# Order of the row maxima and the products with V, in the units that follow a shift

## What is computed

```python
xn = jax.nn.silu(group_norm(x, gn_scale, gn_offset))
qkv = jnp.einsum('bxyc,cd->bxyd', xn, w_qkv)
q, k, v = jnp.split(qkv, 3, axis=-1)          # then to 8 heads of 64 channels
q = q * HEAD_CH ** (-0.5)
sim = jnp.einsum('bhdi,bhdj->bhij', q, k)
attn = jax.nn.softmax(sim, axis=-1)
out = jnp.einsum('bhij,bhdj->bhid', attn, v)  # then heads back to channels
out = jnp.einsum('bxyd,dc->bxyc', out, w_out) + b_out
return out + x
```

## Time and profile before

| | us |
|---|---|
| median of 3 runs (4330.1 to 4330.94) | 4330.39 |
| the profiled execution | 4330.27 |
| its span, from the first to the last instruction | 4328.5 |
| TensorE busy in it | 3827.5 (88%) |
| VectorE busy | 3022.1 (70%) |
| ScalarE busy | 2851.5 (66%) |
| GpSimd busy | 1717.7 (40%) |
| mean granted clock of TensorE | 0.958 |

### The profile page before, as it was taken

How to read it: one execution, slowest core, us unless ns; L and a number is a source line. 1 busy time by engine, 2 the same in 40 slices (tenths; PEclk the granted TensorE clock), 3 DMA queues, 4 the chain that set the end, 5 groups by cost and what they waited for, 6 DMA issues and landing times.

```text
span 4328.5 us, 90413 instructions
## 1 busy us (share of the span) xinstructions
PE 3827.5 (88%) x32844; PEld 2133.3 (49%) x32844; DVE 3022.1 (70%) x3936; ACT 2851.5 (66%) x3202; POOL 1717.7 (40%) x1226
## 2 busy tenths in 40 slices
PE   3889999898998989989899998989989899898997
PEld 1445545454554545545455454545545455454553
DVE  5676676867767676676766768677676766767664
ACT  2676676767767676676766767667676766766664
POOL 1243443433434343343434434334343333434333
PEclk8989999999999999999999999999999999999999
DMA  2111112122021121212111121220311212121111
GB/s 75 37 38 47 57 30 74 31 59 60 16 82 36 50 55 32 73 30 59 45 47 57 30 74 31 59 59 16 82 37 50 55 31 74 30 59 45 40 54 36
DMA packets 105031, 211.25 MB, mean 49 GB/s; under 512 B 13392, under 2 KB 13392, under 8 KB 104656
## 3 DMA queue, kind: packets, MB, share of 16 engines
q1 hardware_dynamic: 104656, 205.84, 17.8%
HBM read 71.57 MB, written 33.55 MB: 24 GB/s over the span
## 4 chain that ended last, share of the span: by engine, by line
PE 52%; DVE 19%; issue 16%; ACT 4%; POOL 4%; SPq 2%; DMA 2%; DVEq 1%; POOLq 0%; ACTq 0%
PE SD L891 27%; PE PV L1004 9%; DVE Pl L760 5%; DVE mx L707 5%; PE TP L905 5%; PE ST L971 4%; PE ST L970 4%; POOL Pl L460 3%; SPq L353 2%; DVE work L750 2%; ACT QK L521 2%; DMA work<-in_x 1%; PE TP L912 1%; ACT Ph L562 1%; PE SD L947 1%
## 5 line engine op out<-in xcount | busy, mean ns | idle before, releaser
L559 ACT ACTIVATE P<-ST,cns 128x1024 f32<-128x1024 f32 x1024 | 1142.0, 1115 | 753.6 <-PE ST L971 536.3
L460 POOL TENSOR_TENSOR Pl<-P,Ph 128x1024 f16<-128x1024 f32 x512 | 1212.0, 2367 | 920.4 <-ACT Ph L562 917.3
L707 DVE TENSOR_REDUCE mx<-TP 128x1 f32<-128x1024 f32 x1024 | 1248.3, 1219 | 234.0 <-PE TP L905 223.8
L562 ACT ACTIVATE Ph<-ST,cns 128x1024 f16<-128x1024 f32 x1024 | 1134.8, 1108 | 0.0
L1004 PE MATMUL PV<-V,Ph 128*128 128x129 f16 (+2 forms) x10240 | 893.7, 213 | 133.9 <-DVE Pl L760 122.8
L1004 PEld LDWEIGHTS PV<-V,Ph 128*128 128x128 f16 x10240 | 790.6, 99 | 385.0 <-DVE Pl L760 150.7
L1004 PE MATMUL PV<-V,Pl 128*128 128x65 f16 x8192 | 861.9, 195 | 0.0
L970 PE MATMUL ST<-QK 128*128 128x512 f16 x2048 | 807.3, 394 | 0.4
L971 PE MATMUL ST<-QK 128*128 128x512 f16 x2048 | 807.1, 394 | 0.0
L1004 PEld LDWEIGHTS PV<-V,Pl 128*128 128x128 f16 x8192 | 740.1, 100 | 89.7 <-issue 17.1
L905 PE MATMUL TP<-QK 128*128 128x512 f16 x2048 | 640.6, 396 | 105.4 <-DVE QK L711 53.8
(11 more groups left out here) (91 smaller groups left out, 2889.6 us busy)
## 6 DMA issues: line engine op xcount, KB each, us to landing
QK<-QK SPq DMA_DIRECT2D x384, 256.0 KB, 4.8
work<-in_x SPq DMA_DIRECT2D x128, 256.0 KB, 2.8
res<-in_x SPq DMA_DIRECT2D x128, 256.0 KB, 2.8
out<-res SPq DMA_DIRECT2D x128, 256.0 KB, 2.0
V<-in_L_conv_w_qkv SPq DMA_DIRECT2D x1, 3072.0 KB, 10.4
P<-in_L_conv_w_out SPq DMA_DIRECT2D x1, 1024.0 KB, 12.3
bias<-in_L_conv_b_out SPq DMA_DIRECT2D x1, 256.0 KB, 7.4
gam<-in_L_conv_gn_scale SPq DMA_DIRECT2D x1, 2.0 KB, 12.0
```

What stands on the lines that cost most here:

```text
L460: nc.gpsimd.tensor_tensor(Pl[:, v % 4, :], P32[:, v % 2, :], Ph[:, v % 4, :], ALU.subtract).then_inc(lo_pool, 1)
L559: nc.scalar.activation(P32[:, v % 2, :], ST[:, v % 2, :], ACT.Exp, scale=cns[:, 0:1])
L562: nc.scalar.activation(Ph[:, v % 4, :], ST[:, v % 2, :], ACT.Exp, scale=cns[:, 0:1]).then_inc(exp_done, 1)
L707: nc.vector.reduce_max(mx[:, hh, qb:qb + 1], TP[:], AX.X).then_inc(top_drained, 1)
```

## The change

The order on TensorE is turned round in the units for which `shift_before` gives a shift, that is, where the unit before ended with one. There TensorE now does the products with V of unit v-2 first and the row maximum of v behind them. Nothing is added or removed, and no other engine's program is touched: `shift_before` is an existing function (L72).

```diff
@@ -1012,11 +1012,14 @@
                     before = (b, v - 2) if v >= 2 else (b - 1, UNITS + v - 2)
                     scores(b, v, 0, cnt)
                     scores(b, v, 1, cnt)
-                    for use in unit_max(s, u, last):
+                    maxima_first = not shift_before(s, u, last)
+                    for use in unit_max(s, u, last) if maxima_first else []:
                         top_use(use, image_of_tops(b, s, u), cnt)
                     if not (first and v < 2):
                         times_v(*before, 0, cnt)
                         times_v(*before, 1, cnt)
+                    for use in [] if maxima_first else unit_max(s, u, last):
+                        top_use(use, image_of_tops(b, s, u), cnt)
                     for use in side_uses(s, u, first, last):
                         side(use, image_of(use, b, s), cnt)
                     for use in unit_shift(s, u, last):
```

## The result

The changed kernel takes 4722.82 us (median of 4 runs, 4712.88 to 4724.11), against 4330.25 us for the kernel before in the same comparison: a ratio of 1.090, with a 95% interval of 1.088 to 1.092. It is 392 us slower. I had forecast 93 us.

The account below looks back on a forecast made before the run. The prediction took the slackless chain of row maximum, reduction, low part and next products as the bound; 15 images at 5.6 us (84 us) plus 9 us for image 15 made 93 us, forecasting 4423 us, range 4385 to 4452.

Parts of the forecast that it names:

- What bounds the kernel: Chain from TensorE's row maximum through VectorE's reduction and low part to TensorE's next products, claimed to have no slack.
- The gain of a plain unit and the 0.62 us: Plain unit: TensorE's 0.09 us wait for the shift copy goes; row maximum and reduction come 0.62 us later.
- The sum: All units together: 5.6 us in each of images 0 to 14, 9 us in image 15, together 93 us.
- unit 23: Would pay 0.62 us, but a 4.77 us wait for an image block two units on takes it up: 0.
- units 43 and 44: Unit 43, at half clock: products end about 0.4 us late, minus 0.25 of slack, counted as +0.2 us.
- Unit 39: Products fit in front of the row maximum's 1.82 us wait for the late shift copy; counted as -0.69 us.
- It ends 0.62 us later.: VectorE's low part of v-1, in order behind the delayed reduction, was claimed to end 0.62 us later.
- units 15 and 35: A projection covers the delay; unit 15 has 2.0 us of slack and gains 0.09 us, unit 35 counts nothing.
- The bounds of the unit's price: Price per delayed unit: at least 0.53 us (79 us in all), at most 0.71 us (106 us).
- the rival: TensorE's clock: lengthened waits add half-clock time, 24 us, giving 4447; chance 0.23 for the clock to either side.
- Faster: Wait for the shift copy goes and the later reduction costs nothing: 53.8 us gained, 4276; chance 0.06.
- nothing measurable: Waits elsewhere (load, placement, statistics) take up the delays; time stays at 4330; chance 0.05.

Follow-up runs that it names:

- turns_on_after: Changed kernel plus a wait: in units with v % 4 = 3 GpSimd's low part starts only after VectorE's of the unit before; 4367.08 us, ratio 1.009.
- turns_on_before: Kernel before plus a wait: in units with v % 4 = 3 GpSimd's low part starts only after VectorE's of the unit before; 4276.91 us, ratio 0.988.
- turns_only_unit7: Kernel before with GpSimd's low part waiting for VectorE's low part of the unit before in unit 7 of each image alone; 4276.9 us, ratio 0.988.

## Why the prediction was wrong

**What bounds the kernel.** Right. The chain (row maximum, reduction, low part, products of the next unit) was the one that decided, and it had no slack.

**The gain of a plain unit and the 0.62 us.** Right. The row maximum starts 1.57 us into the unit and the reduction 2.20, and the next products come 4.62 us behind the start where no turn is lost.

**The sum.** 93 us forecast, 90 us measured, as the difference between `turns_on_after` and `turns_on_before`. That it is so close is partly luck: the sum held the clock as it was, but the clock moved between the two (see below), and the four runs of `turns_on_after` lie 15 us apart. The single units are the better test, by the scores' starts in the two traces, as means over images 1 to 14. Without units 25 and 26 and 33 to 35, where the load wait and stretches at the lower level fall, an image is 6.1 us longer; the sum gives 6.2 for the same units, with unit 23 at 0.62. With all units it is 4.8 us, where I had 5.6. Units 47 and 48 together keep their length, the delay of unit 23 is taken up by the wait for the image block in unit 25, and units 43 and 44 together lose 0.14 us (I had 0.2). Unit 39 gave 0.46 us, not 0.69.

**The step that failed** is this one: "It ends 0.62 us later." I moved VectorE's low part by 0.62 us and kept its duration at 1.22 us. A duration from a row holds only as long as the instruction meets the same neighbours. Here it started 0.08 us behind GpSimd's in place of 0.53 us ahead, and took 3.12 us in place of 1.22. That is 1.9 us more in eleven units of an image. In units 15 and 35 most of it is hidden by a projection, and in unit 23 the wait for the image block takes it up. The other eight pay it: 8 x 16 x 1.9 = 243 us. Unit 15 still pays 0.65 us, 10 us in all. In image 15 all sixteen low parts of these units are long, and the image is 41 us longer, not the 15 counted here, a part of it by the clock. The runs give 4722.8 - 4367.1 = 356 us for all of it. The rest goes in the main with TensorE's clock, as the next point but one argues.

**The bounds of the unit's price** were therefore too narrow. I bounded it by 0.53 and 0.71 us, both from TensorE's rows, and asked only how long others would wait for VectorE. What VectorE itself would wait for inside an instruction was not in the list. The trace of the kernel before had it twice: the low part of GpSimd at 2.68 us in place of 2.12 just behind VectorE's, and the copy of V at 3.17 us. The first has no term in my sum, and I counted the copy as a fixed link in unit 7.

**The clock.** With the turns set right the granted clock was 0.968 in the old order and 0.978 in the new one, 82 us fewer at the lower level, worth up to 41 us. So the order in itself did not bring more of the lower level, although it lengthens ten gaps an image, and the rival was wrong as I had put it. The 90 us above are the order's price less what this gave back. The gaps of lost turns did bring more. The changed kernel has 0.949, that is (1 - 0.949) x 2 x 4721.5 = 482 us in the lower state, against (1 - 0.978) x 2 x 4356.9 = 192 us with the turns set right. Those 290 us are worth up to 145, enough for the 100 us or so that unit 15 and the eight leave open; that they fill it exactly isn't shown. Unit 4 is such a place; in the changed kernel the window from about the start of its products (us, busy by engine, granted clock), first in image 6 and then in image 7:

```profile
1855.90:1859.30 3.40, 3.40 (x23) 1.82 (x21) 1.42 (x2) 1.84 (x2) 0.00 (x0) 0.51 0.00 0
2141.19:2144.59 3.40, 3.40 (x30) 1.83 (x28) 1.41 (x2) 1.99 (x3) 0.00 (x0) 1.00 0.00 0
```

Both follow the same idle time of 2.43 us before the products. In eleven of the sixteen images the clock falls there, and the unit takes 9.0 us or more; in five it stays, and the unit takes 7.39. In `turns_on_after`, where the longest wait for this low part is 0.9 us, it stays in all sixteen, with 5.49 us in most. So the fall comes only with the long wait here, but the wait alone doesn't decide it; what does is open. The Trainium skill's "TensorE: Matmul & The Clock Gate" ("Why this matters for your kernels") advises against long gaps between bursts of matmuls. The trace agrees in eleven images and not in the other five.

**The other rivals.** Faster and nothing measurable both fell with the sum.

**The whole difference**, step by step between measured kernels: before to `turns_on_before` -54 us (one lost turn at the copy of V, and the clock), from there to `turns_on_after` +90 (the order, less what the clock gave back), from there to the changed kernel +356 (the turns lost at the low part, and the clock). Together +392.

## What to carry to other kernels

Before an instruction of VectorE or GpSimd is moved in time, look at what the other one is running at its new place, and give the price of both orders: the one that comes second can take the rest of the first on top of its own length. Here that was so for two subtractions with two SBUF inputs each, and for a copy within SBUF beside such a subtraction. An instruction whose longest duration is far over its median, or whose every execution is longer than in another kernel, may be a lost turn, and a wait on the engine that isn't on the path may win it back; here one such wait gave 1.2%. The time between a start and the start it must not miss belongs in the sum as a term with a threshold, here 0.5 us.

## What the runs showed that I had not expected

- VectorE and GpSimd took turns, whole instruction by whole instruction: 0.21 us ahead VectorE kept its 1.22 us and GpSimd took 2.99; 0.06 us behind it took 3.14 and GpSimd 2.12.
- A wait added on GpSimd made the kernel before 1.2% faster.
- The added reductions from SBUF, with one input, took 0.41 and 0.67 us. The second of them ended 0.14 us behind GpSimd's start, so no run here shows how such a reduction does beside it.
- The time at the lower clock level was about 364 us in the kernel before, 282 in `turns_only_unit7`, 192 in `turns_on_after` and 482 in the changed kernel. All four issue the same matmuls.
